# A graph-network kernel on one core: gathered columns shared out anew between GpSimd and SyncE, chunks of 24 edges, and a search in groups of three

## What is computed

```python
# layer 0: an MLP on every edge, summed per receiver
h = relu(layernorm(x))
x = x + h + segment_sum(silu(silu(e @ W1 + b1) @ W2 + b2) * sigmoid(silu(e @ G1 + g1) @ G2 + g2), dst)
# layer 1: attention over the edges of each receiver, 4 heads of 16
h = relu(layernorm(x))
s, r = h @ Ws + bs, h @ Wr + br
se, re = s[src], r[dst]                       # a gather of one row of 64 floats for every edge
logits = sum_d(mish(se + re) * aw) + ab       # 4 per edge
alpha = softmax of logits over the edges of each receiver
x = x + segment_sum(alpha * se, dst)
```

## Time and profile before

| | us |
|---|---|
| median of 3 runs (5588.56 to 5596.59) | 5589.13 |
| the profiled execution's own time | 5588.17 |
| its span, from the first to the last instruction | 5586.3 |
| edge stage | 0 to about 1147 |
| node stage | to about 1438 |
| attention stage | to about 5442 |
| final stage | to 5586 |

### The profile page before, as it was taken

The page is one execution under the profiler, slowest core; times in us unless marked ns, Lnnn a source line. Parts: engine busy times, 40 slices in busy tenths (PEclk is TensorE's granted clock), DMA queues, the critical chain, the costliest instruction groups (busy, mean ns, idle before and its releaser), DMA issues. The chain is left out here.

```text
span 5586.3 us, 60375 instructions
## 1 busy us (share of the span) xinstructions
PE 1122.8 (20%) x8383; PEld 506.7 (9%) x8383; DVE 4277.6 (77%) x3855; ACT 2852.8 (51%) x3329; POOL 3636.8 (65%) x3692
## 2 busy tenths in 40 slices
PE   7999999923000000000000000000000000000000
PEld 3333344412000000000000000000000000000000
DVE  6888887854477878787878887888787878787871
ACT  7888899911244444444444444444454545454540
POOL 3555300067677777777777777777777777777756
PEclk9999999955555555555555555555555555555555
DMA  7887877721233333332323232323333332323222
GB/s 220 241 254 246 262 252 253 249 53 42 69 79 87 81 85 82 84 89 77 89 77 89 77 89 77 89 78 88 80 86 84 83 89 77 90 77 90 77 64 49
DMA packets 313920, 629.30 MB, mean 113 GB/s; under 512 B 116089, under 2 KB 119584, under 8 KB 313306
## 3 DMA queue, kind: packets, MB, share of 16 engines
q1 hardware_dynamic: 193594, 501.26, 27.8%
q0 software_dynamic: 117968, 125.88, 11.4%
q10 hardware_dynamic: 2128, 0.23, 0.1%
HBM read 391.86 MB, written 235.11 MB: 112 GB/s over the span
## 5 line engine op out<-in xcount | busy, mean ns | idle before, releaser
L933 POOL DMA_INDIRECT se<-s_proj,idx x2058 | 1943.8, 945 | 627.6 <-issue 627.6
L933 POOL DMA_INDIRECT r_se<-s_proj,idx x1050 | 991.4, 944 | 320.3 <-issue 320.3
L989 ACT ACTIVATE held_ps<-exin 128x100 f32<-128x100 f32 x129 | 33.2, 258 | 2139.5 <-DVE z L1052 2131.6
L1191 PE MATMUL a_ps<-r_ident,r_state 128*4 128x128 f32 x1 | 0.4, 372 | 4038.7 <-DVE drop L1220 4038.7
L1052 DVE TENSOR_TENSOR z<-se,held_ps 128x1600 f32<-128x1600 f32 x86 | 243.7, 2834 | 353.2 <-DMA se<-s_proj,idx 329.2
L418 DVE TENSOR_TENSOR_SCAN sums<-keepb,sums,msg 128x1024 f32<-128x1024 bf16 x201 | 472.5, 2351 | 31.3 <-DVE msg L409 27.3
L1087 DVE TENSOR_TENSOR_SCAN work_ps<-work_ps,wse 128x1700 f32<-128x1700 f32 x129 | 478.1, 3707 | 4.4
L340 ACT ACTIVATE hidden<-h_ps,r_b1g 128x1024 f32<-128x1024 f32 x404 | 457.8, 1133 | 9.9 <-PE h_ps L285 9.9
L1039 DVE TENSOR_TENSOR_SCAN held_ps<-held_ps,rnew 128x1600 f32<-128x1600 f32 x129 | 451.3, 3499 | 4.5
L661 POOL DMA_INDIRECT agg<-sums,r_last x98 | 104.3, 1064 | 523.1 <-POOLq L82 493.5
L296 PE MATMUL v_ps<-hidden,r_w2g 64*64 64x512 f32 x1616 | 440.8, 614 | 13.8 <-issue 3.3
(11 more groups left out here) (195 smaller groups left out, 4810.4 us busy)
## 6 DMA issues: line engine op xcount, KB each, us to landing
states<-arows SPq DMA_DIRECT2D x129, 900.0 KB, 7.3
edges<-in_edge_attr SPq DMA_DIRECT2D x202, 512.0 KB, 4.7
rs<-sums SPq DMA_DIRECT2D x129, 800.0 KB, 5.5
sums<-rows SPq DMA_DIRECT2D x402, 256.0 KB
fetched<-s_proj SPq DMA_DIRECT2D x5376, 0.2 KB
keepb<-keep SPq DMA_DIRECT2D x404, 128.0 KB, 3.3
se<-s_proj,idx POOLq DMA_INDIRECT x2058
r_se<-s_proj,idx POOLq DMA_INDIRECT x1050
```

The lines of the kernel that those rows point to most:

```text
L933: pool.indirect_dma_start(out=se[b][:, k, :], out_offset=None, in_=D["s_proj"], in_offset=bass.IndirectOffsetOnAxis(ap=node[:, k:k + 1], a ...
```

## The change

Three edits that come together.

**The layout.** T = 4 and TA = 24 take the place of 25 and 25. RUN becomes 3,224 columns, CA = 135 chunks: 134 of 24 columns and a last one of TL = 8. All operations of attention take the width of their chunk. The padding of `sums` is written from 86 partitions with 128 values each instead of 100 with 192.

**The share of SyncE.** A loop body is now ROUND * B = 9 chunks, and in nine chunks SyncE fetches four columns (PATTERN), each into a tile of its own with a semaphore of its own. The loops turn SB = 14 times, after a first body of three chunks and ahead of two last ones. There are PICKS = 14 * 4 + 2 = 58 columns instead of 42 for SyncE. Step by step SyncE issues 5, 5 and 6 pieces in the first body, then 3, 4, 3, 4, 3, 4, 3, 4, 4 pieces (32) in a turn of the loop, and none in the last six chunks. The wait for an empty tile stands ahead of each column and is for the use of that tile four columns earlier.

**The search.** Q = 3 and NC = 102: 34 rounds of three columns instead of 25 of four, over 36 bodies.

The core of the diff (the operations on VectorE and ScalarE stay the same ones, with the chunk's width):

```diff
-T = 25
+T = 4
-PAD_P = 100
+PAD_P = 86
-Q = 4
-NC = 100
+Q = 3
+NC = 102
-TA, B = 25, 3
-CA = RUN // TA
+TA, B = 24, 3
+CA = -(-RUN // TA)
+TL = RUN - (CA - 1) * TA
-PICK, GANG, COLS = 1, 16, 1
+GANG = 16
+PATTERN = [(0, 1), (1, 0), (1, 2), (2, 1)]
+NPICK = len(PATTERN)
+ROUND = 3
+SB = (CA // B - 3) // ROUND
+PICKS = SB * NPICK + 2
...
+def column_of(m):
+    s, j = divmod(m, NPICK)
+    u, b = PATTERN[j]
+    return (Body(s, u).chunk(b) + 1) * TA - 1
...
-        fetched = sb("fetched", [P, COLS, F])
+        fetched = [sb(f"fetched{j}", [P, F]) for j in range(NPICK)]
-        fetched_in = sem("fetched_in")
+        fetched_in = [sem(f"fetched_in{j}") for j in range(NPICK)]
...
+            def fetch(s, pieces):
+                for piece in pieces:
+                    ahead, j, g = piece // (NPICK * P // GANG), piece // (P // GANG) % NPICK, piece % (P // GANG)
+                    m = (s + ahead) * NPICK + j
+                    if g == 0 and not (isinstance(m, int) and m < NPICK):
+                        sp.wait_ge(placed, m + 1)
+                        sp.sem_inc(sp_turn, 1)
+                    sp.reg_load(nodes, R["picks"][g:g + 1, bass.ds(m, 1), :].rearrange("a i q -> a (i q)"))
+                    for q in range(GANG):
                         node = sp.snap(nodes[q], min_val=0, max_val=NN - 1)
+                        sp.dma_start(fetched[j][g * GANG + q:g * GANG + q + 1, :], D["s_proj"][bass.ds(node, 1), :]).then_inc(fetched_in[j], 16)
+            def body(at, last=False):
+                first, whole = at is FIRST, at.s == SB if isinstance(at.s, int) else False
                 for b in range(B):
                     if not last:
                         sp.wait_ge(carried, c + 1)
                         load(c + B, b)
                     if not (first and b < 2):
                         store(c - 2, (b + 1) % B)
-                    if not last:
-                        if b == 0 and not first:
-                            sp.wait_ge(placed, i)
-                            sp.sem_inc(sp_turn, 1)
-                        fetch(i + 1, PIECES[len(PIECES) * b // B:len(PIECES) * (b + 1) // B])
+                    lot = P // GANG
+                    if first:
+                        fetch(0, range(2 * lot * b // B, 2 * lot * (b + 1) // B))
+                    elif not whole:
+                        n = at.u * B + b
+                        fetch(at.s, [2 * lot + k for k in range(NPICK * lot * n // (ROUND * B), NPICK * lot * (n + 1) // (ROUND * B))])
...
-            body(0, first=True)
-            with sp.Fori(1, NI - 1) as i:
-                body(i)
-            body(NI - 1, last=True)
+            body(FIRST)
+            with sp.Fori(0, SB) as s:
+                for u in range(ROUND):
+                    body(Body(s, u))
+            body(LAST_TWO[0])
+            body(LAST_TWO[1], last=True)
...
-                for k in range(EARLY if first and b == 0 else 0, TA if first or b != PICK else TA - COLS):
+                for k in range(EARLY if first and b == 0 else 0, TA - 1 if at.picks(b) else width(c)):
...
-                    if b2 == PICK and not last:
-                        act.wait_ge(fetched_in, i * (16 * P * COLS) + 16 * P * COLS)
-                        nc.scalar.activation(se[b2][:, TA - COLS:TA, :], fetched[:, :, :], ACT.Copy).then_inc(placed, 1)
+                    ahead, _ = at.after(b + 2)
+                    if not (last and b + 2 >= B) and ahead.picks(b2):
+                        j = PATTERN.index((ahead.u, b2))
+                        act.wait_ge(fetched_in[j], ahead.s * (16 * P) + 16 * P)
+                        nc.scalar.activation(se[b2][:, TA - 1, :], fetched[j][:, :], ACT.Copy).then_inc(placed, 1)
```

More of the change, by code:

```diff
@@ L653, in _ @@
             sp.wait_ge(src_in, 48)
-            sp.wait_ge(picks_in, 16 * COLS * (2 * (CA // B) - LAST // B))
+            sp.wait_ge(picks_in, 16 * (PICKS + sum(column_of(m) + (P - 1) * RUN >= E for m in range(PICKS))))
             for b in range(2):
@@ L863, in attention @@
         NI = CA // B
[L865 to L871, removed]
+        rs_d = D["sums"][0:P * RUN, :].rearrange("(p k) f -> p (k f)", p=P)
+        st_d = D["states"][0:P * RUN, :].rearrange("(p k) f -> p (k f)", p=P)
         @block.sync
@@ L882, in _ @@
+                sp.dma_start(st_d[:, bass.ds(c * (TA * ROW), w * ROW)], rows[b][:, 0:w, :].rearrange("p k f -> p (k f)")).then_inc(stored[b], 16)
             nodes = [sp.alloc_register(f"node{g}") for g in range(GANG)]
[L884 to L890, removed]
+            def fetch(s, pieces):
[7 more added lines that the diff above has]
+                    for q in range(GANG):
@@ L895, in body @@
                 for b in range(B):
-                    c = i * B + b
+                    c = at.chunk(b)
                     if not last:
@@ L924, in _, with gather @@
         def _(pool):
-            def gather(i, b, first=False):
-                c = i * B + b
+            def gather(at, b):
+                c, first = at.chunk(b), at is FIRST
                 if not first:
@@ L938, in _ @@
             for b in range(B):
-                gather(0, b, first=True)
-            with pool.Fori(1, NI) as i:
+                gather(FIRST, b)
+            with pool.Fori(0, SB) as s:
+                for u in range(ROUND):
+                    for b in range(B):
+                        gather(Body(s, u), b)
+            for at in LAST_TWO:
                 for b in range(B):
-                    gather(i, b)
+                    gather(at, b)
             for b in range(B):
-                pool.wait_ge(gathered[b], landed(NI - 1, b))
+                pool.wait_ge(gathered[b], LAST_TWO[1].landed(b))
         @block.scalar
@@ L975, in mish_tail, with body @@
                 wait(act, rows_ready, c * 2)
-                nc.scalar.activation(act_ps, t1[:, :, :], ACT.Exp, scale=-1.0).then_inc(r_ready, 1)
-            def body(i, first=False, last=False):
+                nc.scalar.activation(act_ps(width(c)), narrow(t1, width(c)), ACT.Exp, scale=-1.0).then_inc(r_ready, 1)
+            def body(at, last=False):
                 for b in range(B):
-                    c = i * B + b
+                    c, first = at.chunk(b), at is FIRST
                     b1, b2 = (b + 1) % B, (b + 2) % B
+                    w = width(c)
                     mish_tail(c)
                     if not last:
-                        act.wait_ge(gathered[b], landed(i, b))
+                        act.wait_ge(gathered[b], at.landed(b))
                         index(c + B, b)
@@ L1015, in _ @@
             mish_head(0, 0)
[L1016 to L1019, removed]
+            body(FIRST)
+            with act.Fori(0, SB) as s:
+                for u in range(ROUND):
+                    body(Body(s, u))
+            body(LAST_TWO[0])
+            body(LAST_TWO[1], last=True)
         @block.vector
@@ L1024, in _, with receivers @@
             STEP = 15
[L1026 to L1030, removed]
+            def receivers(at, b, more=True):
+                at, b = at.after(b)
+                c = at.chunk(b)
+                w = width(c)
+                hold, new = rneg(w), narrow(rnew, w)
+                dve.wait_ge(rs_in[b], at.i * 16 + 16)
                 dve.wait_ge(keepf_ready, c + 1)
-                nc.vector.scalar_tensor_tensor(rnew[:, :, :], rneg, 1.0, rs[b][:, :, :].rearrange("p k f -> p f k"),
+                nc.vector.scalar_tensor_tensor(new, hold, 1.0, rs[b][:, 0:w, :].rearrange("p k f -> p f k"),
                                                ALU.subtract, ALU.mult).then_inc(rnew_ready, 1)
@@ L1054, in body, with add_senders @@
-            def body(i, last=False):
+                    nc.vector.tensor_scalar(rlast[:, :], hold[:, :, w - 1], keep0[:, bass.ds(c + 1, 1)], None, ALU.mult).then_inc(rlast_ready, 1)
+            def add_senders(at, b):
+                at, b = at.after(b)
+                c = at.chunk(b)
+                w = width(c)
+                dve.wait_ge(gathered[b], at.landed(b))
+                if at.picks(b):
+                    dve.wait_ge(placed, at.pick(b) + (NPICK + 1))
+                nc.vector.tensor_tensor(narrow(z[b], w), se[b][:, 0:w, :].rearrange("p k f -> p f k"), rneg(w), ALU.subtract).then_inc(z_ready, 1)
@@ L1055, in body @@
+            def body(at, last=False):
                 for b in range(B):
-                    c, before = i * B + b, (b + 2) % B
+                    c, before = at.chunk(b), (b + 2) % B
+                    w = width(c)
+                    mish, lgs, lgs_b, kneg, top, sums = act_ps(w), narrow(lg, w), narrow(lgb, w), narrow(knegf[b], w), narrow(mx[b], w), weighted(w)
+                    steps, fade, exs = step[:, 0:H * w], decin[:, 0:H * w], ex_ps(w)
                     do = Order(dve, chain, c * STEP + PREP)
@@ L1070, in body @@
[L1070 to L1072 removed]
+                    do(nc.vector.tensor_tensor_scan(flat(top), flat(kneg), flat(lgs_b), 0.0, ALU.add, ALU.max))
```

(20 more changed lines are left out.)

160 lines of the change are left out of this document (93 added, 67 removed).

## The result

| | before | after |
|---|---|---|
| median, us | 5588.85 (4 runs) | 5988.96 (4 runs, 5987.13 to 5990.02) |
| profiled execution: time, span | 5588.17, 5586.3 | 5988.55, 5986.6 |
| edge stage ends | 1147 | 1111 |
| a turn of nine chunks of 24 columns | | 299.9 |
| columns that SyncE fetches | 42 | 58 |

The changed kernel takes 1.0713 times as long (95% interval 1.0694 to 1.0731): 400 us more, where 383 were forecast. Two things moved: the edge stage became 36 us shorter, and attention 438 us longer.

A forecast was written before the change was run, and what follows sets the result against it. GpSimd was taken to bound attention before, SyncE's issue queue after, at 297.7 us a turn. Attention +406 us and edge stage -22 on 5588.2 gave 5972 us, range 5880 to 6070, slower at 92%.

The forecast's parts named there:

- Who bounds: Attention: GpSimd's gathers bound the kernel before; after the change SyncE's issuing does, 33 us a turn over GpSimd's need.
- price list: SyncE's issues in attention: a piece 7.92 us, a step 28.40 with three pieces, 36.32 with four, jump back 2.45.
- A turn of SyncE: Attention's loop: four steps of three pieces, five of four and the jump back take 297.7 us; 14 turns 4168.
- SyncE's waits costed at nothing: Attention's loop: SyncE waits for nobody, 0 us; the rival of waits on top, 6250 us, had 4%.
- The start and the end of attention: First fetch at 1452.98 to loop at 1584.3; after the turns, 78 us for bodies 131 to 133 and narrow chunk.
- The edge stage: Search of three columns: 35 us of cost gone, 0.35 us per body (13 us) left, a gain of 22 us.
- GpSimd, VectorE, ScalarE: Attention: GpSimd waits some 30 us a turn for VectorE or ScalarE, held by late receiver rows or picked columns.
- The sum: Whole kernel: 5588.2 + 406 for attention - 22 for the edge stage = 5972 us.

The follow-up runs named there:

- experiments 1: Changed kernel with PATTERN cut to three columns per nine chunks, each with its own tile and semaphore: 5547.42 us, 0.9927 of the kernel before.
- experiment 6: Changed kernel with 14 instead of 16 row transfers in each piece, two rows of every 16 left at zero: 5597.41 us.
- experiment 7: Changed kernel with each step's first register load moved ahead of its issues of receiver rows and store: 5757.48 us.
- 8: Changed kernel with GANG = 32, so 32 node numbers in one register load and 16 loads a turn instead of 32: 5901.09 us.
- 12: Changed kernel with seven columns per eighteen chunks and the first register load ahead, on a usual chip: 5540.54 us, 0.9906 of the kernel before.
- experiments 2: Changed kernel with the search put back to Q = 4, NC = 100: 6020.03 us, 1.0773 of the kernel before.
- 3: Kernel before with Q = 3 and NC = 102 alone: 5554.39 us, 0.9931 of the kernel before.
- experiment 9: Changed kernel with each step's store moved behind its pieces: 8693.85 us, on a chip where the kernel before took 8539.78.
- experiments 9 to 11: Changed kernel with store behind pieces, then seven columns in eighteen chunks with and without first load ahead: 8693.85, 8634.18, 8781.51 us; kernel before 8539.78 there.
- experiment 11: Changed kernel with seven columns per eighteen chunks, steps otherwise as in it: 8781.51 us, 1.0290 of the kernel before on the same chip.
- run 5: Not named so in the kept text; the fifth follow-up is the kernel before with each register load issued twice: 5590.44 us, 1.0001 of it.

## Why the prediction was right, point by point

*Who bounds.* Right. It rested on one waiting time and one price list: 77 us of SyncE's work in a body of 92.4, for one column in three chunks. Eight pieces of 7.92 us are 63 of these 77; a third more of them, with the rest as it was, is 98, over 92 before any detail. The theory stood against five edits that each moved SyncE's work by a known amount (experiments 1, 6, 7, 8 and 12); the time followed within 4 us in three of them, and in the other two the trace shows which price differed.

*A turn of SyncE.* 297.7 forecast, 299.9 measured in the turn shown. The 14 turns together take 4195.2 us (1547.5 to 5742.7), 299.7 each, which is 27 us over the 4168 forecast. No one term was wrong: in the turn shown the steps of three pieces take 28.7 us on average instead of 28.40, those of four 36.4 instead of 36.32, and the jump back 3.0 instead of 2.45 (the step before it takes 39.41), which makes 1.2 + 0.6 + 0.5 us.

*SyncE's waits costed at nothing.* Right: it has none in the loop.

*The start and the end of attention.* From the first fetch to the loop 131.3 forecast, 131.7 measured (1415.8 to 1547.5). From SyncE's last step (5742.7) to the end of the last sums (5838.5) 95.8 instead of 91: ScalarE was still waiting for a store, until 7 us behind the last one's issue, a wait that my sum had at the receiver rows, so that body 131 began 19.3 us behind that step instead of 12.7. The three bodies then took 65.3 us for 63, and the narrow chunk 11.2 for 15. Whether the narrow last chunk gains anything by itself was not tested.

*The edge stage.* A gain of 22 us forecast, 36 measured, of which 32 to 33 are the search's by experiments 2 and 3. The mechanism was the right one, the wait for fetched nodes; the term that was mis-sized is what is left of a round's cost, put at 0.35 us per body (13 us) and in fact 2 to 3 us in all. VectorE's work for the search is real but fits beside the pace of the blocks.

*GpSimd, VectorE, ScalarE.* GpSimd waits 33 us a turn, 30 had been named. The middle of the chain was wrong: I had named receiver rows and picked columns as what comes late, and it is the stores. It made no difference to the sum, because SyncE's queue is one order in which all of them are late together.

*The sum.* 5972 against 5989: +27 for the turns, +5 for the end of attention, -2 for the final stage, and -15 for what lies ahead of attention. That the total is nearer than its largest term is luck, since the two large errors have opposite signs. The range was added up too narrowly: by its own terms the upper end is 5972 + 84 + 33 + 15 = 6104, and not 6070. The measured time lies in either.

## What to carry to other kernels

A sequencer that only issues transfers shows no busy time, but it has a capacity like any engine: add up its issues by the price between two starts, look for steps that follow each other without a wait, and compare the sum with the period of whoever bounds the loop. Here one row transfer costs SyncE 0.42 us and one column 64 us, to spare GpSimd 1.25 us: this pays only out of SyncE's idle time, and ends in a cliff. With the search of three alone the kernel takes 5554 us, with the new layout and three columns in nine chunks 5547, with three and a half (and the load first) 5541, with four 5989. When everything behind such a queue is late, a long wait for something in it need not name the cause, only one of the items that come late; changing the amount of another item in it (experiment 6) tells the two apart. And an experiment that adds work should be checked in the trace for the work being there.

## What the runs showed of the hardware that I had not expected

**What stands behind a store on SyncE's queue is slow.** A register load of 16 that follows the issue of a 128-partition store takes 3.0 to 4.2 us in the changed kernel (median 3.9) instead of 1.13: 127 of the 464 loads, one for every step with a store, and no other takes over 1.4. Where rows follow the store instead (experiment 7), they take 1.1 us longer for 48 of them. Behind the issue of a load alone it is not long: in the earlier trace rows the first fetch follows the end of the piece before it by 1.8 us, with an issue of receiver rows between. In the run with the store ahead of the load of the next step, the row transfers begin about 4 us after the store's issue too, in whatever order the rest stands (trace of experiment 9, SyncE's timeline):

```profile
6170.61 0.39 SPq L946 DMA_DIRECT2D states<-arows  x1
6171.32 0.36 SPq L941 DMA_DIRECT2D rs<-sums  x1
6174.53 81.68 SPq L961 DMA_DIRECT2D fetched<-s_proj  x64
```

At a loop end of that run 5 us pass between the store and the issue of receiver rows (6029.33 to 6034.46), and there the rows begin 2.0 us behind the latter, which leaves no room for a long load. Why a store holds up what follows isn't shown.

**On one chip SyncE was slow in spells.** On the chip of experiments 9 to 11 SyncE's 64 rows of a step took 81.68 us, as above, while its steps of 48 rows next to them took the usual 23. It isn't the length of the step: in experiment 11 a step of 48 rows took 73.54 us and the next one, of 64, 31.02. In the slow spells single rows start 4.2 us apart (the usual distance is 0.42); the other engines' instructions have their usual lengths, and the two stages before attention, which issue little through SyncE, end only 46 us later together (the first row is fetched at 1461.9, in the changed kernel at 1415.8). The kernel before, too, took 8540 us there; no trace of it was taken on that chip, so that it was bound by SyncE there is an inference. The cause is open. It doesn't go by the number of columns alone: on that chip 42 columns (the kernel before) took 8540 us and 58 (experiment 9) 8694.
